# Sorting the attention result by DMA instead of transposing it there and back

## The reference

```python
Q, K, V = split_heads(x @ Wq.T + bq), split_heads(x @ Wk.T + bk), split_heads(x @ Wv.T + bv)   # 16 heads of 8
scores = einsum('bhid,bhjd->bhij', Q, K) / sqrt(8)
scores = where(j > i, -inf, scores) - (i - j)          # causal, linear decay
attn = softmax(scores, axis=-1)
out = einsum('bhij,bhjd->bhid', attn, V)               # back to (B, T, 128)
x = layernorm(x + out @ Wo.T + bo)
h = silu((x @ w1.T) * w1_s) * ((x @ w2.T) * w2_s)      # 128 -> 512, ternary weights
h = gelu((h @ h1.T) * h1_s); h = gelu((h @ h2.T) * h2_s)
x = layernorm(x + (h @ w3.T) * w3_s)
```

## Time and profile before

| | |
|---|---|
| median of 3 executions | 789.07 us |
| the profiled execution's own time, and its span | 788.52 us, 786.8 us |
| busy, share of the span: PE, DVE, ACT, POOL | 94%, 78%, 71%, 62% |
| fill (to PE's wait for the flag) | 0 to 99.3 us |
| 14 slots | 99.3 to 729.4 us |
| drain | 729.4 to 786.8 us |

### The profile page before, as it was taken

The page is one execution under the profiler, slowest core; times in us unless marked ns, Lnnn a source line. Parts: engine busy times, 40 slices in busy tenths (PEclk is TensorE's granted clock), DMA queues, the critical chain, the costliest instruction groups (busy, mean ns, idle before and its releaser), DMA issues. The chain is left out here.

```text
span 786.8 us, 19041 instructions
## 1 busy us (share of the span) xinstructions
PE 742.4 (94%) x6218; PEld 508.8 (65%) x6218; DVE 610.6 (78%) x2887; ACT 561.0 (71%) x908; POOL 487.4 (62%) x584
## 2 busy tenths in 40 slices
PE   3678999999999999999999999999999999999995
PEld 1455566676767676676767666676767667675763
DVE  3978878787978878797878878797887979787232
ACT  5055858778695967768686877869596776868775
POOL 4164365667575665667576566757656566757764
PEclk8558999999999999999999999999999999999997
DMA  7510302112030301103030211203030120300000
GB/s 215 174 30 5 112 2 83 46 45 85 16 113 2 117 14 60 70 16 114 16 113 2 88 41 50 80 16 114 2 115 15 60 70 3 114 3 30 1 1 29
DMA packets 26540, 44.91 MB, mean 57 GB/s; under 512 B 3240, under 2 KB 6632, under 8 KB 26440
## 3 DMA queue, kind: packets, MB, share of 16 engines
q1 hardware_dynamic: 26440, 43.67, 16.2%
HBM read 12.20 MB, written 4.19 MB: 21 GB/s over the span
## 5 line engine op out<-in xcount | busy, mean ns | idle before, releaser
L949 DVE CUSTOM_DVE_ANT_0 ps<-ps,causal 128x256 f32<-128x256 f32 x960 | 308.3, 389 | 44.4 <-PE ps L610 43.7
L1146 POOL TENSOR_TENSOR hlo<-hf,hhi 128x512 fp32r<-128x512 f32 x128 | 164.1, 1293 | 128.3 <-ACT hhi L883 128.3
L793 ACT ACTIVATE pt<-ps 128x768 f32<-128x768 f32 x256 | 194.7, 807 | 38.9 <-PE ps L648 34.8
L1107 POOL TENSOR_SCALAR_AFFINE_SELECT pt<-pt 128x512 f32<-128x512 f32 x256 | 160.0, 639 | 92.9 <-ACT pt L793 88.8
L873 ACT ACTIVATE hf<-ps,vec_sb 128x512 f32<-128x512 f32 x128 | 88.1, 688 | 111.6 <-PE ps L568 110.2
L562 PE MATMUL ps<-hhi,h_hi 128*128 128x512 f32 x496 | 146.9, 417 | 0.3 <-ACT hhi L883 0.3
L568 PE MATMUL ps<-hlo,h_hi 128*128 128x512 f32 x496 | 134.1, 391 | 0.3 <-POOL hlo L1146 0.3
L949 DVE DVE_READ_ACCUMULATOR2_ANT m<- 128x1 f32 x960 | 131.6, 137 | 0.0
L568 PEld LDWEIGHTS ps<-hlo,h_hi 128*128 128x128 f32 x496 | 93.1, 188 | 23.6 <-POOL hlo L1146 1.2
L665 PE MATMUL ps<-pt,vst 128*32 128x256 f32 (+1 forms) x2048 | 105.6, 337 | 0.3 <-POOL pt L1107 0.3
L562 PEld LDWEIGHTS ps<-hhi,h_hi 128*128 128x128 f32 x496 | 84.1, 188 | 20.2 <-issue 3.0
(11 more groups left out here) (121 smaller groups left out, 1132.7 us busy)
## 6 DMA issues: line engine op xcount, KB each, us to landing
qs<-q_hi SPq DMA_DIRECT2D x30, 256.0 KB
ks<-k_hi SPq DMA_DIRECT2D x30, 256.0 KB
...
```

The source lines that it names most:

```text
L793: nc.scalar.activation(pt[u][:, c:c + 2, :], ps[:, first:last + 1, 0:3 * P], ACT.Exp).then_inc(t_free.sem, 1)
L949: part = nc.vector.tensor_tensor_reduce(ps[:, bank, cols], ps[:, bank, cols], mask, 1.0, LOWEST, ALU.add, ALU.max, m32[b][:, it, c + e, u: ...
L1107: nc.gpsimd.affine_select(out=diag, in_=diag, compare_op=ALU.is_ge, fill=0.0, base=0, pattern=[[0, 2], [0, 2], [1, P]], channel_multiplier ...
L1146: nc.gpsimd.tensor_tensor(h_lo[layer % 2][:, m, :], hf[:, n % 4, :], h_hi[layer % 2][:, m, :].bitcast(F32), ALU.subtract).then_inc(hlo_rea ...
```

## The change

The transposes are gone on both sides. In `vst` the eight V columns of a head are now every second column, and the eight between them are all ones: the product then has eight numerator rows and eight equal rows of sums, interleaved. Four DMAs for each half (`repack`, 64 partitions x 256 elements each) copy the even rows of `raw` to `num` and the odd rows to `den`, so that each holds 128 features of 256 tokens, in an order that the rows of `Wo` are permuted to beforehand. `arec` (DVE) takes the reciprocal of `den`, 128x256; `amul` (POOL) multiplies `num` by it into `attT`. `atr`, `atT` and `attT`'s copy fall away, `anorm` becomes `arec` and `amul`.

Beside this, pair 0's second half (b = 1) now goes through `s1`/`smax1`, head by head, instead of `s`/`smax`. All tables are written anew.

```diff
-                    ("atr", 0): [(attn_ready, 4)], ("atr", 1): [(attn_ready, 8)],
-                    ("atT", 0): [(attT_ready, 1)], ("atT", 1): [(attT_ready, 2)],
...
+                    elif kind == "repack":
+                        _, b, odd, half = s
+                        raw_ready.wait(sp, q, b + 1)
+                        attT_ready.wait(sp, q - 1, b + 1)
+                        carry(sp, "sp")
+                        sp.dma_start((num, den)[odd][64 * half:64 * half + 64, b * T:(b + 1) * T],
+                                     raw[odd::2, half * T:(half + 1) * T]).then_inc(repacked.sem, 16)
...
-                        elif kind == "atr":
-                            raw_ready.wait(pe, q, s[1] + 1)
-                            for j in range(4):
-                                last = pe.transpose(ps[:, ONE, j * P:(j + 1) * P], raw[:, j * P:(j + 1) * P],
-                                                    ident[:])
-                            last.then_inc(at_full.sem, 1)
-                        elif kind == "atT":
-                            attn_ready.wait(pe, q, 4 * s[1] + 4)
-                            for j in range(2):
-                                last = pe.transpose(ps[:, ONE, j * P:(j + 1) * P], attn[:, j, :], ident[:])
-                            last.then_inc(at_full.sem, 1)
...
-                            if (b, n, e) == (0, 0, 0):
+                            if (q, n, e) == (0, 0, 0):
+                                pe.wait_ge(half_stacked[1], 16 * 7)
+                            elif (b, n, e) == (0, 0, 0):
                                 stacked.wait(pe, 0)
...
-                        nc.scalar.copy(attT[:, b * T:(b + 1) * T], ps[:, ONE, 0:T]
-                                       ).then_inc(attT_ready.sem, 1)
...
-                        nc.vector.memset(vst[i][:, j, odd::2, :, 16 * odd + HD:16 * odd + HD + 1],
+                        nc.vector.memset(vst[i][:, j, odd::2, :, 16 * odd + 1:16 * odd + 16:2],
                                          1.0).then_inc(vst_ones, 1)
...
-                        nc.vector.reciprocal(rec[:], rv[:, :, :, :, HD]).then_inc(rec_ready.sem, 1)
...
+                        repacked.wait(dve, q, 4 * b + 4)
+                        nc.vector.reciprocal(den[:, b * T:(b + 1) * T], den[:, b * T:(b + 1) * T]
+                                             ).then_inc(rec_ready.sem, 1)
...
+                    elif kind == "amul":
+                        b = s[1]
+                        l_full.wait(pool, q - 1, 1)
+                        carry(pool, "pool")
+                        rec_ready.wait(pool, q, b + 1)
+                        nc.gpsimd.tensor_tensor(attT[:, b * T:(b + 1) * T], num[:, b * T:(b + 1) * T],
+                                                den[:, b * T:(b + 1) * T], ALU.mult).then_inc(attT_ready.sem, 1)
...
 PE_ORDER = [
-    ("s", 0, 0, 0), ("pv", 1, 1, -1), ("pv", 1, 2, -1), ("s", 0, 1, 0), ("s", 0, 2, 0), ("atT", 0, -1),
+    ("s", 0, 0, 0), ("pv", 1, 2, -1), ("s", 0, 1, 0), ("s", 0, 2, 0), ("pv", 1, 3, -1), ("h", 1, 0, -2),
...
 DVE_ORDER = [
-    ("smax", 0, 0, 0), ("gmul", 3, -2), ("smax", 0, 1, 0), ("smax", 0, 2, 0), ("smax", 0, 3, 0),
-    ("anorm", 1, -1), ("smax", 0, 4, 0), ("smax", 0, 5, 0), ("smax", 0, 6, 0), ("smax", 0, 7, 0), ("res1", -1),
+    ("gmul", 3, -2), ("smax", 0, 0, 0), ("smax", 0, 1, 0), ("smax", 0, 2, 0), ("arec", 0, -1),
+    ("smax", 0, 3, 0), ("smax", 0, 4, 0), ("smax", 0, 5, 0), ("arec", 1, -1), ("smax", 0, 6, 0),
```

More of the change, by code:

```diff
@@ new lines @@
+    ("exp", 0, 1, 1), ("table", "exp", -1), ("exp", 0, 2, 1), ("exp", 0, 3, 1), ("exp", 0, 4, 1),
+    ("exp", 0, 5, 1), ("lnnorm", 1, 0), ("x1hi", 0), ("x1c", 0), ("tanh", 0, 0), ("qhi", 0, 2),
+    ("exp", 0, 6, 1), ("tanh", 1, 0), ("qhi", 1, 2), ("ghi", 0, 0), ("exp", 0, 7, 1), ("tanh", 2, 0),
+    ("exp", 1, 0, 1), ("exp", 1, 1, 1), ("tanh", 3, 0), ("exp", 1, 2, 1), ("exp", 1, 3, 1), ("exp", 1, 4, 1),
+    ("ghi", 1, 0), ("exp", 1, 5, 1), ("exp", 1, 6, 1), ("ghi", 2, 0), ("exp", 1, 7, 1), ("ghi", 3, 0),
@@ L113 @@
-    ("w_mx", 1), ("gmul", 2, 0), ("gate", 3, 0), ("anorm", 0, 1),
[4 rows of a table added]
+    ("smax1", 1, 7, 1, 1), ("w_mx", 0), ("x1lo", 0), ("gate", 0, 0), ("qlo", 0, 2), ("gmul", 0, 0),
+    ("gate", 1, 0), ("qlo", 1, 2), ("mTc", 1, 1), ("mTl", 1, 1), ("gate", 2, 0), ("araw", 0, 1), ("gmul", 1, 0),
+    ("vadd", 2), ("gmul", 2, 0), ("gate", 3, 0), ("w_mx", 1),
 ]
 POOL_FILL = [
-    ("w_lo", 0), ("w_lo", 1), ("sel", 0, 0, 0), ("sel", 0, 1, 0), ("sel", 0, 2, 0), ("sel", 0, 3, 0),
-    ("sel", 0, 4, 0), ("sel", 0, 5, 0), ("sel", 0, 6, 0), ("sel", 0, 7, 0), ("sel", 1, 0, 0), ("sel", 1, 1, 0),
@@ new lines @@
+    ("smax", 0, 3, 0), ("smax", 0, 4, 0), ("smax", 0, 5, 0), ("arec", 1, -1), ("smax", 0, 6, 0),
+    ("smax", 0, 7, 0), ("res1", -1), ("smax", 1, 0, 0), ("lnstat", 1, -1), ("smax", 1, 1, 0), ("mTc", 0, 0),
+    ("mTl", 0, 0), ("smax", 1, 2, 0), ("smax", 1, 3, 0), ("smax", 1, 4, 0), ("smax", 1, 5, 0), ("x1lo", -1),
+    ("smax", 1, 6, 0), ("smax", 1, 7, 0), ("qlo", 0, 1), ("gate", 0, -1), ("gmul", 0, -1), ("qlo", 1, 1),
+    ("res2", -2), ("mTc", 1, 0), ("mTl", 1, 0), ("gate", 1, -1), ("gmul", 1, -1), ("gate", 2, -1),
@@ L194 @@
+    ("gelu", 2, 0, -1), ("hhi", 2, 0, -1), ("gelu", 2, 1, -1), ("hhi", 2, 1, -1), ("gelu", 2, 2, -1),
+    ("hhi", 2, 2, -1), ("gelu", 2, 3, -1), ("hhi", 2, 3, -1),
 ]
 DVE_DRAIN = [
-    ("gmul", 3, -2), ("anorm", 1, -1), ("res1", -1), ("lnstat", 1, -1), ("x1lo", -1), ("gate", 0, -1),
-    ("gmul", 0, -1), ("gate", 1, -1), ("gmul", 1, -1), ("gate", 2, -1), ("gmul", 2, -1), ("gate", 3, -1),
-    ("gmul", 3, -1), ("res2", -2), ("lnstat", 2, -2), ("lnnorm", 2, -2), ("res2", -1), ("lnstat", 2, -1),
@@ L199 @@
-    ("lnnorm", 2, -1),
+    ("arec", 0, -1), ("gmul", 3, -2), ("arec", 1, -1), ("res1", -1), ("lnstat", 1, -1), ("x1lo", -1),
+    ("gate", 0, -1), ("gmul", 0, -1), ("gate", 1, -1), ("gmul", 1, -1), ("gate", 2, -1), ("gmul", 2, -1),
+    ("gate", 3, -1), ("gmul", 3, -1), ("res2", -2), ("lnstat", 2, -2), ("lnnorm", 2, -2), ("res2", -1),
+    ("lnstat", 2, -1), ("lnnorm", 2, -1),
 ]
 POOL_DRAIN = [
-    ("glo", 3, -2), ("xbo", -1), ("hlo", 1, 0, -2), ("hlo", 1, 1, -2), ("hlo", 1, 2, -2), ("hlo", 1, 3, -2),
@@ L210 @@
 ]
-ONE_KINDS = ("qq", "qk", "qv", "mT", "atr", "atT", "wo", "zt", "x1t")
+ONE_KINDS = ("qq", "qk", "qv", "mT", "wo", "zt", "x1t")
 FULL_SLOTS = range(2, PAIRS)
@@ L406, in gated, with wait_max, first_max @@
             return pt[m][:].rearrange("p c k -> p (c k)")[:, 0:TOK] if q == LAST else hf[:, m, :]
-        def max_pair(q):
-            return max(q - 1, 0)
+        def wait_max(signal, eng, q, k):
+            signal.wait(eng, max(q - 1, 0), k - HP if q else k)
+        def first_max(q, b, n, e=0):
+            return 2 * HP * (2 * q + b - 1) + 2 * n + e
         def proj_bank(q, kind):
@@ L417, in wait_max_banks @@
             if i >= 2:
-                s_free.wait(eng, max_pair(q), i - 1)
+                wait_max(s_free, eng, q, i - 1)
             else:
@@ L434, in wait_exp_banks @@
             elif i < 2:
-                s_free.wait(eng, max_pair(q), 2 * HP - 1 + i)
+                wait_max(s_free, eng, q, (2 * HP if q else HP) - 1 + i)
             else:
@@ L1183 @@
     order = np.arange(D).reshape(U, C, HD).transpose(1, 2, 0).reshape(-1)
+    rows = np.arange(D).reshape(2, 2, C, HD).transpose(0, 2, 1, 3).reshape(-1)
     def tiles(w):
```

170 lines of the change are left out of this document (71 added, 99 removed), and 89 rows, old and new, of tables (DVE_FILL, PE_DRAIN, PE_FILL, PE_ORDER).

## The result

| | before | changed |
|---|---|---|
| median of 8 runs | 788.39 us | 792.00 us |
| profiled execution, and its span | 788.52, 786.8 us | 793.55, 791.8 us |
| DVE's copy of the first half's raw rows in the first full slot | 142.06 us | 154.65 us |
| the same copy for the last pair | 725.88 us | 728.76 us |

The ratio is 1.0046, with a 95% interval of 1.0035 to 1.0058: slower by about half a per cent, where the forecast was 786.0 us and faster. One of the eight executions before took 2161.72 us; without it their median is 788.33 us. The copy of the raw rows happens once a slot, so it parts the 5.0 us of span: up to the first full slot +12.6 us, the 13 slots to the last copy -9.7 us (44.16 against 44.91 us each), and behind it +2.1 us (63.04 against 60.92). The slots did what was forecast, and more. Both ends lost it.

What follows compares the result with a forecast made beforehand. PE sets the pace in a slot's first stage, with DVE only 2.6 us to spare. From 788.5 us, slots -7, fill +5.5 and drain -1.5 gave 785.5, stated as 786 us; range 771 to 797 us.

Steps and rivals of the forecast that it cites:

- The slots: Fourteen slots: each falls from 44.89 to 44.4 us, -7 us in all.
- The reciprocal: New DVE step, two per slot: 1.80 us each, with 1.33 to 2.84 us left open by the rows.
- The first stage: Slot up to the first `st`: 26.6 us of PE plus 0.5 + 0.1 + 0.3 + 0.3 of waits and delays, 27.8 us.
- the `pv` for the `atr`: Slot's second stage: a moved `pv` of 0.76 us replaces the 0.76 us `atr`, so the stage stays at 16.6 us.
- start: Fill: DVE starts 4.4 us late and later idle time takes back about half; 2.2 us lost.
- path: Fill, from `raw`'s end to `wo`: 3.6 us become 6.9 us, 3.3 us more.
- slack: Fill, first `g`: it stood behind a `qq` and the last `s1`, so 2 us are taken off.
- behind: Fill, from first `g` to the flag: steps moved there make 14.4 us some 16.5, 2.1 us more.
- The drain: End of the kernel: transposes and a moved `pv` go, new path about as long as four `h` groups; -1.5 us.
- PE as the only bound: Rival, slots: DVE's idle time absorbs the reciprocals; slot 43.2 to 43.7 us, time 769 or 776 us; chance 0.20.
- DVE as the bound: Rival, slots: reciprocal of 2.1 to 2.3 us, slot 45.0 to 45.4 us, slower at 794 to 800 us; chance 0.20.
- The free fill: Rival, fill: late start is taken back and earlier `exp` offset the longer path; 780 us; chance 0.15.

Runs made afterwards that it cites:

- pv_back: Changed kernel with one product step, pv(1,1), moved back behind the first score step of the next slot, in fill, slots and drain; 798.7 us.
- short_reciprocal: Changed kernel with the reciprocal run over only the first 32 of its 256 columns; 779.1 us.
- pv_ahead: Changed kernel with last gate product before the drain's first reciprocal, six half-0 score steps first in the fill, and pv(1,3) before each slot's third score step; 787.4 us.
- drain_gmul: Changed kernel with one drain step moved: DVE takes the last gate product ahead of the first reciprocal; median 788.63 us, ratio to before 1.0011.
- path_alone: Changed kernel's new attention path, slots and drain, with the fill order of the kernel before; median 790.64 us, ratio 1.0028.
- path_and_ends: Changed kernel with the old fill order, the drain's gate product ahead of the first reciprocal, and separate semaphores for denominators and numerators; 787.94 us.
- reduces_early_gap: Changed kernel with drain gate product first, six half-0 score steps first, u(2) in the fill's gap, and DVE's weight-remainder reductions early; median 785.86 us.
- final: Changed kernel with drain gate product first, half-0 scores first, fill gap filled by u(2), reductions early, denominators on their own semaphore; median 784.82 us, ratio 0.9956.
- raw_other_buffer: Changed kernel with pair 0's second-half raw rows in their own buffer in the fill, and a repack semaphore for each half; median 791.88 us.
- den_first: Changed kernel with drain gate product first, six half-0 score steps first, and repacked denominators and numerators on separate semaphores; median 785.61 us, ratio 0.9962.

## Why the prediction was wrong

**The slots were right in number, in part by luck.** The reciprocal was forecast at 1.80 us and took 1.744; the product took 0.739 for 0.75. The first stage was 27.95 us for 27.8, with a wait of 0.48 for 0.5 at the third `s`. The second was 16.26 for 16.6: I held it for PE's, and took the `pv` for the `atr` as an even exchange, but pv_back shows that what PE does there isn't its limit. A slot came to 44.2 for 44.4, and the 14 slots gave 7.7 us for 7, by what the 5.0 us of span leave beside fill and drain (10.6 + 2.1 - 5.0). I built the first stage as PE's work plus waits; short_reciprocal shows that DVE's work counts in it as well. That the 0.5 us for the wait belongs in the sum isn't shown: filling it, in pv_ahead, gained nothing.

**The fill failed, most of all in one term.** My four terms can be read off the rows:

| | forecast | measured, changed less before |
|---|---|---|
| start: copy of the second half | 2.2 | 70.37 - 68.14 = 2.2 |
| path: copy to `wo` | 3.3 | 8.55 - 4.20 = 4.35 |
| slack: `wo` to `g` | -2 | 10.53 - 12.51 = -2.0 |
| behind: `g` to the flag | 2.1 | 20.46 - 14.43 = 6.0 |
| sum | 5.6 (I wrote 5.5) | 10.6 |

The step that failed is "14.4 us (84.85 to 99.28) grow to some 16.5": it became 20.46. drain_gmul, whose fill table is the same, took 17.86, and its PE timeline parts the rest (first the changed kernel, then drain_gmul):

```profile
92.64 0.33 PE L662 MATMUL ps<-qs,ks 32*128 32x128 f32 x2
```

```profile
90.53 0.80 PE L576 MATMUL ps<-x1hi,w_hi 128*128 128x512 f32 x1
...
92.77 0.33 PE L662 MATMUL ps<-qs,ks 32*128 32x128 f32 x2
...
104.53 0.33 PE L662 MATMUL ps<-qs,ks 32*128 32x128 f32 x2 [0.84 <-ACT pt L797]
...
108.39 0.19 PE L760 MATMUL ps<-ones_col,lo_all 128*1 128x1 f32 x2
```

- The head. The first `g` matmul took 0.50 us before (84.85) and 0.80 in the changed kernel: PE was still at half clock, 0.50 from 80 to 90 us, where the kernel before had 0.75 from 80 to 85 and 1.00 from 85 on. Its busy time was 3.30 us of 80 to 85 and 3.13 of 85 to 90, that of the kernel before 4.85 and 5.00; whether the clock hung on that is not shown. From `g` to the first `st` the changed kernel took 3.19 us and drain_gmul 2.24; at full clock throughout I estimate 1.74 (0.80 for the three matmuls of that `g`, 84.85 to 85.65 in the kernel before, and 0.94 for `qq`, 91.83 to 92.77 in drain_gmul, at 1.00 in both). So, by that estimate, 1.45 us are the clock, which I had taken for full.
- The second fall of the clock, for which I had no term. From the `st` at the gap to the flag: 109.91 - 104.43 = 5.48 us against 3.86 in drain_gmul, where the clock was 1.00 up to the flag: 1.6 us.
- What is left, 20.46 - 14.43 - 1.45 - 1.62 = 3.0 us, is the steps that moved behind `g`, where I had 2.1. In path_alone, where one `pv` more stands behind `g`, the transposes of `raw` are gone and the clock was full throughout, the stretch was 15.61 us.

The second fall goes on behind the flag. From the flag to the copy in the first full slot the changed kernel took 44.74 us; the four profiled executions in the same slot order whose clock stayed at 1.00 there (path_alone, path_and_ends, reduces_early_gap, final) took 41.74 to 41.79. That is 3.0 us more, and 4.6 for the whole fall in the profiled execution, nearly its 5.0 us of span. The lower group isn't free of a fall either: drain_gmul and raw_other_buffer, profiled there, fell behind 112 us (0.50 from 113 to 115 us, 1.00 again from 116 on) and took 43.20 and 43.14 us, 1.4 more. Without it the changed kernel would lie, by my estimate, at 790.2 - 1.4 = 788.8 us, about where it was before: by that estimate the half per cent is for the most part this clock, and the rest of the fill and the drain used up what the slots gave.

In the path, four issues took 2.65 us (71.05 to 73.70) for 2.6, and the second reciprocal started 2.5 us behind them, where I had 1.4 for the landing. That isn't a landing time: it shows no wait, since DVE had the first reciprocal and maxima to do until then. In short_reciprocal it did wait, and began 1.5 us behind the last issue (SP's and DVE's timelines):

```profile
72.47 2.10 SPq L556 DMA_DIRECT2D num<-raw  x2
...
76.09 0.35 DVE L986 RECIPROCAL den<-den 128x32 f32<-128x32 f32 x1 [0.67 <-DMA num<-raw]
```

So by this row the landing was priced well, and the path's extra 1 us is DVE's own queue, which my sum of the path left out.

**The drain had the wrong sign.** I took the new path for "about as long as the four `h` groups ahead of it" and didn't follow DVE's table, where `gmul` stands behind `arec`. That order cost 2.5 us. With it mended the sentence holds: `wo` follows the `h` groups, and den_first's second reciprocal, 1.3 us earlier, did not move it. But the drain is then 0.3 us shorter than before, not 1.5. PE's timeline, before and in drain_gmul:

```profile
732.02 1.20 PE L562 MATMUL ps<-hhi,h_hi 128*128 128x512 f32 x4
...
740.21 1.05 PE L686 MATMUL ps<-wo_sb,attT 128*128 128x128 f32 x8
```

```profile
731.22 0.86 PE L681 MATMUL ps<-pt,vst 128*32 128x256 f32 x16 [0.68 <-POOL pt L1093]
732.01 1.19 PE L576 MATMUL ps<-hhi,h_hi 128*128 128x512 f32 x4
...
739.63 1.05 PE L690 MATMUL ps<-wo_sb,attT 128*128 128x128 f32 x8
```

From the first `h` to `wo` it is 7.62 us instead of 8.19: the two transposes that stood between the `h` groups. What went ahead of the first `h` gave nothing: PE now waits there for masks, and that `h` starts 6.39 us behind the copy, 6.14 before. I had counted 1.6 us of PE's steps as saved without asking which of them PE waited behind anyway.

**The rivals.** PE as the only bound needed a slot of 43.2 to 43.7 us; even with the reciprocals cut to an eighth it was 43.77. DVE as the bound came near in time (794 to 800) and not in cause: its condition, a reciprocal above 1.9 us, wasn't met. No run shows the 2.1 to 2.3 us that it reckoned with; the 32 reciprocals of the changed kernel took 1.744 us in the mean. The free fill (780 us) fell with the flag, 10.6 us later. That is outside my own +1 to +9 us for the fill too, and so the sum of 785.5 missed the profiled 793.55 by 5.1 in the fill and 3.6 in the drain, less 0.7 in the slots. The measured median lies inside the range of 771 to 797, by the width that the second rival gave it.
